# The node table of a two-layer graph kernel stored as three bf16 parts per row

## The reference

```python
# layer 0: a gated edge network, summed by src
z = concat([x[src], x[dst], edge]) @ W.T + b           # then batch norm over the edges
agg = zeros.at[src].add(sigmoid(z[:, :H]) * softplus(z[:, H:]))
x1 = layernorm(x + (x + agg))
# layer 1: the mean of the neighbours, by dst
msg_sum = segment_sum(x1[src], dst); cnt = segment_sum(1, dst)
gain = tanh(norm(x1 - msg_sum / max(cnt, 1)))
enhanced = relu(x1 @ W1 + b1) @ W2 + b2
h = x1 + 0.2 * enhanced * gain
out = layernorm(x1 + (layernorm(h) * gamma + beta))
```

## Time and profile before

| | us |
|---|---|
| median of three runs | 3951.27 |
| the profiled execution | 3949.06 |
| its span, first to last instruction | 3947.3 |
| POOL busy | 2695.6 (68%) |
| PE busy | 3027.4 (77%) |
| DVE busy | 2949.3 (75%) |
| ACT busy | 2222.9 (56%) |

### The profile page before, as it was taken

How to read it: one execution, slowest core, us unless ns; L and a number is a source line. 1 busy time by engine, 2 the same in 40 slices (tenths; PEclk the granted TensorE clock), 3 DMA queues, 4 the chain that set the end, 5 groups by cost and what they waited for, 6 DMA issues and landing times. The chain is left out here.

```text
span 3947.3 us, 81199 instructions
## 1 busy us (share of the span) xinstructions
PE 3027.4 (77%) x17192; PEld 2107.0 (53%) x17193; DVE 2949.3 (75%) x7793; ACT 2222.9 (56%) x6111; POOL 2695.6 (68%) x2634
## 2 busy tenths in 40 slices
PE   6865888888888999999999966767774477666652
PEld 2321444444436777777777745556663355455541
DVE  8998899989985555455454538999996589778857
ACT  1422999999985666666666659989993000000003
POOL 3887777777776777777777740048888777777770
PEclk8976999999999999999999987888887788888876
DMA  7332333333335888888888894457763222222232
GB/s 202 117 101 88 105 97 104 98 104 100 102 98 176 263 261 263 261 260 262 263 259 263 261 243 177 186 209 274 267 241 121 86 74 79 79 78 78 73 50 38
DMA packets 314706, 637.18 MB, mean 161 GB/s; under 512 B 54382, under 2 KB 188567, under 8 KB 306551
## 3 DMA queue, kind: packets, MB, share of 16 engines
q0 software_dynamic: 99440, 246.26, 22.6%
q1 hardware_dynamic: 172984, 266.56, 21.0%
q10 hardware_dynamic: 42192, 123.38, 8.3%
HBM read 423.94 MB, written 212.05 MB: 161 GB/s over the span
## 5 line engine op out<-in xcount | busy, mean ns | idle before, releaser
L367 POOL DMA_INDIRECT rec_d<-arena x830 | 886.0, 1068 | 311.2 <-issue 310.9
L853 POOL DMA_INDIRECT arena<-b_tab,arena x880 | 838.6, 953 | 292.1 <-issue 257.9
L767 PE MATMUL psum<-arena 128*128 128x440 f16 x3360 | 675.7, 356 | 34.9 <-ACT arena L461 33.3
L874 DVE TENSOR_TENSOR arena<-psum,arena 128x512 f32<-128x512 f32 x440 | 284.6, 686 | 551.5 <-DMA arena<-b_tab,arena 310.2
L964 PE MATMUL psum<-weT,arena 128*128 128x256 f32 x1760 | 548.7, 394 | 55.7 <-DVE arena L874 52.1
L461 ACT ACTIVATE arena<-arena 128x128 f16<-128x128 f16 x1680 | 561.7, 386 | 0.0
L626 DVE TENSOR_SCALAR arena<-iota_t,arena 128x880 f16<-128x880 f16 x840 | 500.8, 661 | 51.9 <-PE psum L767 49.3
L767 PEld LDWEIGHTS psum<-arena 128*128 128x128 f16 x3360 | 323.5, 99 | 381.9 <-DVE arena L626 56.3
L1453 DVE TENSOR_TENSOR arena<-psum,arena 128x256 f32 x880 | 372.9, 424 | 156.9 <-PE psum L1573 150.1
L1573 PE MATMUL psum<-x_sb,arena 128*128 128x256 f32 x1152 | 320.9, 439 | 198.7 <-DVE x_sb L1461 85.3
L967 PE MATMUL psum<-arena 128*128 x2640 | 435.1, 274 | 0.0
(11 more groups left out here) (255 smaller groups left out, 5807.2 us busy)
## 6 DMA issues: line engine op xcount, KB each, us to landing
z_d<-arena ACTq DMA_DIRECT2D x220, 512.0 KB
arena<-z_d SPq DMA_DIRECT2D x44, 2560.0 KB
arena<-rec_d SPq DMA_DIRECT2D x220, 260.0 KB
arena<-in_edge_attr SPq DMA_DIRECT2D x83, 640.0 KB, 4.8
arena<-early_d SPq DMA_DIRECT2D x34, 512.0 KB
arena<-b_tab,arena POOLq DMA_INDIRECT x880
rec_d<-arena POOLq DMA_INDIRECT x831, 3.4
early_d<-arena POOLq DMA_DIRECT2D x9, 1024.0 KB, 4.2
```

The source lines that it names most:

```text
L367: nc.gpsimd.indirect_dma_start(rec_rows, bass.IndirectOffsetOnAxis(e_idx[:, s, k:k + 1], 0), e_buf[:, s, k, :], None).then_inc(s_es[s], 16)
L767: last = nc.tensor.matmul(bank(4 + 2 * k + h)[:, 0:HALF], hot_lane[:, s, k, :], hot_tile[:, s, h * HALF:(h + 1) * HALF], start=start, stop ...
L853: nc.gpsimd.indirect_dma_start(bg[:, s, k, :], None, b_tab, bass.IndirectOffsetOnAxis(rec[:, s, k, H:H + 1].bitcast(I32), 0)).then_inc(s_b ...
```

## The change

- Each row of `x1_tab` becomes three bf16 parts (high, middle, low; their sum is the f32 value): 768 bytes instead of 512. `early_d`, the ring and the early buffer `xb` grow by half. The blanking of the table at the start grows from 3136 KB to 4704 KB, in two transfers.
- The parts of the 16 early blocks are made by four DVE operations over 128x2048 at the end of `normalise_early`.
- The parts of all 49 blocks are made in four pieces of 12 or 13 blocks: ACT rounds to the high part, DVE subtracts it, ACT rounds the rest to the middle part, DVE subtracts again. SP stores each piece in a transfer of its own. The clearing of `sumT` moves behind that, and the addition of `beta` waits until the last piece is stored.
- The one-hots of the second gather are bf16, and PE multiplies three times per tile (one bf16 product per part, accumulated) instead of once in f32.
- Before every fourth early gather POOL waits until `s_fl` shows that enough message groups have been added: the first burst of four at 77, and two more for each following burst.
- All four slots of the ring lie where `x` was; before, two of them did.

```diff
-        x1_tab = nc.dram_tensor("x1_tab", (ROWS + EARLY_BLOCKS * P, H), F32).ap()
-        early_d = nc.dram_tensor("early_d", (P, EARLY, G * H), F32).ap()
+        x1_tab = nc.dram_tensor("x1_tab", (ROWS + EARLY_BLOCKS * P, ROW), BF16).ap()
+        early_d = nc.dram_tensor("early_d", (P, EARLY, G * ROW), BF16).ap()
...
-                for i, part in enumerate(PARTS):
-                    sp.wait_ge(s_x1w, i + 1)
-                    sp.wait_ge(s_x1a, i + 1)
-                    sp.dma_start(x1_tab[0:ROWS, :].rearrange("(b p) f -> p b f", p=P)[:, part, :], x1[:, part, 0:H]).then_inc(s_xs, 16)
+                for i, part in enumerate(SPLITS):
+                    sp.wait_ge(s_hi, i + 1)
+                    sp.wait_ge(s_mid, i + 1)
+                    sp.wait_ge(s_lo, i + 1)
+                    sp.dma_start(x1_tab[0:ROWS, :].rearrange("(b p) f -> p b f", p=P)[:, part, :],
+                                 x1p[:, part, :, :].rearrange("p b k f -> p b (k f)")).then_inc(s_xs, 16)
...
+                BURST = 4
+
+                def first_added(k):
+                    return EARLY_TILES // YG + 2 + 2 * (k // BURST)
...
                     for k in range(G):
+                        if k % BURST == 0:
+                            pool.wait_ge(s_fl, first_added(g * G + k))
                         nc.gpsimd.indirect_dma_start(ring_slot(g % XS)[:, k, :], None, x1_tab,
...
-                pool.wait_ge(s_xs, 48)
+                pool.wait_ge(s_xs, X1_STORED)
...
                     norm0.act_scale(i, agg, x1f, s_x1a)
+                    for j in (2 * i, 2 * i + 1):
+                        act.wait_ge(s_x1w, i + 1)
+                        act.wait_ge(s_x1a, i + 1)
+                        nc.scalar.activation(x1p[:, SPLITS[j], 0, :], x1[:, SPLITS[j], 0:H], ACT.Copy).then_inc(s_hi, 1)
+                    for j in (2 * i, 2 * i + 1):
+                        act.wait_ge(s_left, j + 1)
+                        nc.scalar.activation(x1p[:, SPLITS[j], 1, :], less[:, SPLITS[j], :], ACT.Copy).then_inc(s_mid, 1)
...
-                    last.then_inc(s_x1e, 1)
+                    early(last)
+                    row = x1e[:, :, 0:H]
+                    early(nc.vector.tensor_copy(x1ep[:, :, 0, :], row))
+                    early(nc.vector.tensor_tensor(row, row, x1ep[:, :, 0, :], ALU.subtract))
+                    early(nc.vector.tensor_copy(x1ep[:, :, 1, :], row))
+                    nc.vector.tensor_tensor(x1ep[:, :, 2, :], row, x1ep[:, :, 1, :], ALU.subtract).then_inc(s_x1e, 1)
...
-                nc.vector.memset(sumT, 0.0)
...
+                for j, part in enumerate(SPLITS):
+                    if j == 2:
+                        dve.wait_ge(s_x1a, 2)
+                    dve.wait_ge(s_hi, j + 1)
+                    nc.vector.tensor_tensor(less[:, part, :], x1[:, part, 0:H], x1p[:, part, 0, :], ALU.subtract).then_inc(s_left, 1)
+                    if j >= 1:
+                        low(j - 1)
+                low(len(SPLITS) - 1)
+                dve.wait_ge(s_lo, len(SPLITS))
+                nc.vector.memset(sumT, 0.0)
...
+                dve.wait_ge(s_xs, X1_STORED)
                 nc.vector.tensor_tensor(x1b, x1f, gb[:, 1, :].unsqueeze(1).broadcast_to([P, BLOCKS, H]), ALU.add).then_inc(s_xb, 1)
...
-                        nc.tensor.matmul(bank((8 * place + k) % RING)[:, 0:Z], rows[:, k, :], hotg[:, place % 2, k, :], start=True, stop=True).then_inc(s_sg, 1)
+                        for part in range(PARTS3):
+                            last = nc.tensor.matmul(bank((8 * place + k) % RING)[:, 0:Z], rows[:, k, part * H:(part + 1) * H], hotg[:, place % 2, k, :],
+                                                    start=(part == 0), stop=(part == PARTS3 - 1))
+                        last.then_inc(s_sg, 1)
```

More of the change, by code:

```diff
@@ L534, in early_enough @@
                     after(nc.vector.tensor_scalar(early_key, early_src, float(ROWS), None, ALU.mult))
-                    nc.vector.tensor_scalar(need[:], early_src, -32.0, 48.0, ALU.mult, ALU.add)
+                    nc.vector.tensor_scalar(need[:], early_src, 16.0 - X1_STORED, float(X1_STORED), ALU.mult, ALU.add)
                 def windows():
@@ L865, in hots @@
                     for k in range(YG):
-                        last = nc.vector.tensor_scalar(hot[:, s, k, :], iota1b[:], rec[:, s, k, H + 1:H + 2], None, ALU.is_equal)
+                        last = nc.vector.tensor_scalar(hot[:, s, k, :], iota1b, rec[:, s, k, H + 1:H + 2], None, ALU.is_equal)
                     last.then_inc(s_oh, 1)
@@ L1047, in build @@
         x1b = tmp([BLOCKS, H], F32)
+        spare = arena[:, cursor[0] - 2 * BLOCKS * H:cursor[0]]
+        x1p = spare[:, 0:BLOCKS * ROW // 2].bitcast(BF16).rearrange("p (b k f) -> p b k f", k=PARTS3, f=H)
+        less = sumT[:, 0:BLOCKS * H].rearrange("p (b f) -> p b f", f=H)
         hT = tmp([2, 512], F32)
@@ L1441, in _, with low @@
                     norm0.dve_scale(i, agg, x1f, s_x1w)
+                dve.wait_ge(s_x1w, 2)
+                dve.wait_ge(s_x1a, 1)
+                def low(j):
+                    dve.wait_ge(s_mid, j + 1)
+                    nc.vector.tensor_tensor(x1p[:, SPLITS[j], 2, :], less[:, SPLITS[j], :], x1p[:, SPLITS[j], 1, :], ALU.subtract).then_inc(s_lo, 1)
+                for j, part in enumerate(SPLITS):
[8 more added lines that the diff above has]
+                nc.vector.memset(sumT, 0.0)
                 def pairs_of(kind, n):
@@ L1460, in hots_and_adds @@
                         t = first_tile(kind, n) + k
-                        last = nc.vector.tensor_scalar(hotg[:, place % 2, k, :], iota256[:], l1_loc[:, bass.ds(t, 1)], None, ALU.is_equal)
+                        last = nc.vector.tensor_scalar(hotg[:, place % 2, k, :], iota256b[:], l1_loc[:, bass.ds(t, 1)], None, ALU.is_equal)
                         if before is not None:
```

52 lines of the change are left out of this document (32 added, 20 removed).

## The result

The changed kernel takes 3961.11 us (median of 20 runs) against 3949.01 us (20 runs) for the one before: 12 us more by the medians, a ratio of 1.0023 with a 95% interval of 1.0013 to 1.0034, that is some 9 us. The prediction said 3973, 22 us above its own base. The sign was right and the range holds the time, but 9 us is less than half of the 22, and by the bound of 0.5% the outcome is "the same", to which it gave 40 in 100, with 50 for slower. One term of the sum was wrong by more than the whole loss, and the experiments are about that term.

The account below looks back on a forecast made before the run. POOL's chain of gathers from 2612 to 3850 us was taken as the bound, plus the stop: 7.1 + 2 + 11.5 + 1.5 - 1 + 1 = 22.1 us, giving 3971 us for the profiled execution, 3973 as median; range 3960 to 3985.

Parts of the forecast that it names:

- What bounds the kernel: From 2612 to 3850 us the time is one chain of POOL writing gathers; DVE and PE don't limit the second gather.
- The stop: At `normalise_early`, four more DVE operations keep DVE from the messages and delay messages and early gathers alike: +7.1 us.
- The store to the first gather: Early store, from issue to POOL's first gather, grows from 1024 KB to 1536 KB: +2 us (0 to 3.3).
- Pacing: POOL's waits before early gathers under the messages are already fulfilled, since POOL is behind: 0 us.
- The step that failed: After the messages, subtractions and clearing on DVE hold up POOL's remaining early gathers: +11.5 us (5 to 13.5).
- Rival B: The subtractions after the messages don't stall POOL's early gathers: 22.1 less 11.5, so 3962 us; 2 in 10.
- Stores to `early_d`: On POOL's list, only the last store holds POOL, longer at 1.5 MB: +1.5 us (0 to 2.3).
- Direct gathers: In the second gather, 608 at the same price, with 1 us of POOL's waits for PE given back: -1 us.
- The last tiles: At the second gather's end every row asked for is the same, priced per row and not per byte: +1 us.
- Rival C: Last gathers asking for one row are priced by bytes, +16 us more, 3989 us; or dearer descriptors, 12; 15 in 100.
- Rival A: Early gathers become quick, at 1.36 us each, and direct gathers start 24 us sooner: 3927 us; 1 in 10.
- More than 9 us of waits for PE: Sign that the forecast is wrong: POOL waiting this long for PE's products in the second gather.

Follow-up runs that it names:

- pieces without waits: The kernel before, with DVE's message operation of 2560 elements cut into three pieces issued back to back; 3919.54 us against 3947.00, ratio 0.9927.

## Why the prediction was right or wrong

- What bounds the kernel: right. PE's and DVE's work fell in the second gather and nothing followed; POOL's chain from the first early gather sets the end: where it got its last early gather out 41 us sooner (pieces without waits), the kernel became 27.5 us faster. The kernel with only the stop is as slow as the changed one.
- The stop, 7.1 us: measured 7.2. The two-input operations were 2.29 (2.25), the casts 1.23 (1.2). The store to the first gather 1.1 in place of 2.
- Pacing 0: right on a chip like the one of the profile; the changed kernel without it is no different.
- **The step that failed** is "by rows 7 it stands still while DVE works in one piece: 5.0 and 13.9 us in place of the 5.4 us alone", +11.5 us. Three things were wrong in it. The subtractions aren't one piece; each stands behind a wait, and there a gather gets in, at a loss of 0.2 to 0.55 us per gather (1.6 once) and not of the operations' whole length: 4.3 us in all. The clearing was counted in the 13.9 us, but it holds nobody; the copy behind it did, and the change had taken that away. And the 5.4 us to be set against it were thus a gain of 6.65. Net -2.3 where I had +11.5; the table's +0.7 has 3.2 us of scatter under the messages in it. The row that should have warned me was my own of the earlier trace rows: the clearing reads no array, so an explanation by arrays read couldn't cover it.
- Rival B came within 1 us of the time (3962), by luck: the subtractions do hold POOL, 4.3 us of the 11.5. What made the number come out is the clearing, which B doesn't mention. My own range holds the time by luck too, since it was drawn around a term with the wrong sign.
- Stores to `early_d` +1.5: measured +1.2. Direct gathers -1: -3.0. All of it lies in the gathers themselves: POOL's idle time between them is the same 185.4 us, 11.9 of it now put down to PE in place of 9.1, but 34 gathers take over 0.97 us in place of 99, and the mean fell from 959.5 to 954.6 ns; why isn't shown. The last tiles +1: a gather does cost nearly a tenth more there, but the end came 0.7 us sooner, since the products behind the last gathers are shorter (4.49 us for the last group above, before 5.65).
- Rival C, a price by bytes: excluded by 953 ns and by the 1.7 us per gather at the end. Rival A would need gathers below 1.6 us; they stayed at 1.705.
- What the profile was to show: the stop, the 1.7 us per early gather and PE's last group 12 us behind the last gather came. PE's busy time fell by 14% and not by a third. No gather of over 5 us stood beside the pieces (the longest took 2.52) and none of 12 beside the clearing, which is the failed step again. The first direct gather came at 3097.8 and not at 3104, although the messages began 4.65 us late. More than 9 us of waits for PE was to be a sign of being wrong; it came (11.9), but the kernel before has 9.1 already, so it tells nothing. By the earlier trace rows 46 early gathers were left at 3000 us, not 48, which changes nothing.
- The chances: with the failed term at its measured value the same working gives 22.1 - 13.8 = 8.3 us, close to the measured 8 to 9, and "the same" as the likeliest.

## What to carry to other kernels

Where POOL writes descriptors and is late, look at DVE's list for runs of operations that read two arrays or copy, with no wait among them, and at what stands right behind a long harmless one; one copy of 0.17 us, ready behind the clearing, cost POOL 6.6 us here. A wait inserted to let POOL in is paid by DVE (0.24 us each time under the messages, most of it by a load in its list that had been hidden), so it belongs only where DVE has time. And a change that makes a stage cheaper which isn't the limit pays its own costs at the joints in full: here 7 us in the stop at `normalise_early`.

## What the runs showed of the hardware

- A DVE clearing of 5.39 us leaves POOL's gathers at 0.95 to 0.98 us (five traces), but with a copy of 0.17 us ready behind it the gather beside it takes 6.55 to 7.60 us (seven traces) and ends 0.81 or 0.82 us after the copy.
- Two-input DVE operations hold POOL over a run of them as if it were one (7 by 1.08 us: 7.63 us), and one wait between two of them is enough for a gather to get in (1.49 us beside operations of 1.76 us), even one that is fulfilled already and costs DVE no time. With three pieces of an operation back to back under the messages a gather sometimes got in as well; what decides it stays open.
- A load of 1.17 us in DVE's list is hidden (0 to 0.04 us idle behind it) while DVE reads its list ahead under earlier operations, and lies open for 0.61 us or more when a wait keeps DVE from reading ahead.
- An indirect gather of 128 rows costs POOL 953 ns at 512, 768 and 1024 bytes a row. If all 128 ask for the same row, the DMA queue needs 1.56 us at 512 and 1.7 us at 768 bytes, against 0.25 and 0.37 us (29.4% of 40 us for 32 gathers) with different rows.
- On chips where the kernel takes 5.4 to 5.6 ms the messages nearly stood still while POOL wrote gathers that weren't held back (ACT busy 42 of 350 us, DMA share 0.37). That the gathers are the cause isn't isolated.
